# Sparsemax cross-attention and FFN on one core: thresholds tested by exact row sums on ScalarE, projections moved between phases

## The chip, the cores and the metric

One Trainium2 chip, one core of it. The metric is device time in microseconds (us) of one execution, median of several. Engines are named as the profile names them: PE (TensorE), DVE (VectorE), ACT (ScalarE), POOL (GpSimd), SP (SyncE, which here only starts transfers).

## What is computed

Eight batch elements; for each, 100 query rows of width 512 attend over 722 context rows with 16 heads of 32, and a feed-forward block follows. The attention weights are not a softmax but a sparsemax, which needs for every row a threshold tau such that the clipped row sums to one:

```python
def sparsemax(x):
    x = x - jnp.max(x, axis=-1, keepdims=True)
    zs = -jnp.sort(-x, axis=-1)
    cssv = jnp.cumsum(zs, axis=-1) - 1.0
    support = zs > cssv / rho                      # rho = 1, 2, ..., L
    k = jnp.maximum(jnp.sum(support, axis=-1, keepdims=True), 1)
    tau = jnp.take_along_axis(cssv, k - 1, axis=-1) / k
    return jnp.clip(x - tau, 0.0)

x = x + attn(layernorm(x), ctx, ctx, Wq, bq, Wk, bk, Wv, bv, Wo, bo)   # scores * 32**-0.5, sparsemax, @ v, @ Wo
real = layernorm(x) @ cos(theta + theta_noise)
imag = layernorm(x) @ sin(phi + phi_noise)
x = x + sqrt(real * real + imag * imag)
```

## The kernel before, in words

Work goes in half-batches: half `i` holds the 8 heads `8*(i%2)..` of batch element `b = i//2`, so there are 16 halves. Every engine runs its own program in order; they meet at semaphores. The order of work is written out by hand as **phases** `i = -1..17`, and each engine's program has the same loop `for i in PHASES`, with generators that give steps of work and a function `weave` that mixes two of them.

What one half goes through:

- **k, v, q.** PE multiplies the context by `wk2` and `wv2` in three fp16 terms (`three_terms`, L407; 12 matmuls of k or v are one unit of four steps), the normalised x by `wq` in float32 (L445 to L448, after a transpose, L432). ACT reads each result out of PSUM (k twice, as `ks` L605 and `k_f` L609; v, L594, with a cast of the next batch's context, `high_ctx`, right behind it), POOL makes the low fp16 parts (`low_k` L323, `low_ctx` L314, `low_q` L329), SP stacks k in `kst` (`stack_k`).
- **scores(i).** 16 matmuls (L494) give the 8 heads' scores; ACT copies each head to the tile `S` (100x722 float32). `S` holds two halves.
- **maxes(i, h)**, DVE: 12 MAX8 a head (L803) find 96 candidates a row. **thresholds(i)**, DVE: four Newton steps on the candidates of all eight heads (L812 to L837), then a last comparison (L839 to L848) that counts whether the number above tau changed (`n_last`, `n_now`) and whether a piece's eighth candidate is above tau (`n_edge`).
- **sum_flags(i)**, PE: three small matmuls add these counts over the rows into `flag_ps` (L480 to L482). **settle(i)**, DVE: it waits for them, loads their maximum into a register, and if it isn't 0 loops over the eight heads, loads each head's count and refines the heads that are not 0 (`refine`: the row clipped again from `S`, L872, two Newton steps over all 722 elements, L851 to L862, a test whether that was enough). Then it raises `verified`.
- **split_tau(i)**, POOL: after `verified` five small instructions split tau in three fp16 parts (L344 to L352) and raise `tau_split`.
- **attend(i)**, PE: it waits for `tau_split`, transposes the parts (L531), ACT copies them beside q, then six units of transposed scores minus tau (L543), clipped by ACT into `pT` (L711), multiplied with v (L520), woven with k matmuls.
- Then the output projection (`o_of`, L457), the second layernorm, the FFN (L472), `sum_squares`, `root`, `y_of`, and the store.

DVE does half `i` in phase `i`, with `settle(i-1)` after the third head's maxes; PE in phase `i` does `sum_flags(i-1)`, `attend(i-1)` and `scores(i+1)`:

```python
if odd:
    first = chain(q_of(b + 1), k_of(b + 1, 0), k_of(b + 1, 1)) if b + 1 < B else iter(())
    second = ffn_of(b - 1) if 0 <= b - 1 < B else iter(())
else:
    first = chain(k_of(b, 2), k_of(b, 3)) if b < B else iter(())
    second = chain(*vs[0:2], *([o_of(b - 1)] if b > 0 else []), *vs[2:])
```

`first` runs ahead of attend and woven into it, `second` is woven into the scores. In the prologue SP starts all weight transfers, POOL fills constants (L292 to L307), DVE splits the weights and computes the angles of the FFN weights (`angles`).

## Time and profile before

| | |
|---|---|
| median of 3 runs | 979.97 us (978.62 to 981.37) |
| profiled execution, its own time | 981.16 us |
| span in its profile | 979.3 us |
| PE matmuls busy | 600.7 us, 61% |
| DVE busy | 670.2 us, 68% |
| ACT busy | 372.5 us, 38% |
| POOL busy | 185.7 us, 19% |
| mean granted clock of TensorE | 0.803 of full speed |

No engine is busy throughout. The chain that ended last is 39% PE, 24% "issue" (an engine that waits for nothing the profile shows), 18% DVE, 5% ACT, 5% POOL.

### The profile page before, as it was taken

The page shows a single profiled execution, that of the slowest core. Times are in us where ns is not written, and L with a number is a line of the kernel's source. Part 1 is how long each engine was busy: PE and PEld are TensorE (multiplying, and loading weights), DVE is VectorE, ACT ScalarE, POOL GpSimd, SP SyncE. Part 2 cuts the span into 40 slices and gives each one's busy share as a digit, 9 for nine tenths or more (in the row PEclk, how much of TensorE's full clock was granted, in tenths as well). Part 3 has the DMA queues.
Part 4 walks back from the last instruction along what each step waited for, and adds up shares of the span by engine and source line. Part 5 has one row for each costly group of instructions (what it writes and reads, how often), then busy time and mean ns, then how long its engine had stood idle before and what let it go on. Part 6 is the DMA issues. An engine that isn't in the chain of part 4 may idle for free.

```text
span 979.3 us, 14685 instructions
## 1 busy us (share of the span) xinstructions
PE 600.7 (61%) x4592; PEld 354.0 (36%) x4592; DVE 670.2 (68%) x2683; ACT 372.5 (38%) x605; POOL 185.7 (19%) x223
## 2 busy tenths in 40 slices
PE   0556716319619097379747960979155498793675
PEld 0233304106305064246434630555042354462442
DVE  7169957659549494689569964996476787694731
ACT  1242324206306054255425540645143354642231
POOL 9523201002200122012301230022110032110000
PEclk9967857659959699598969995989678698987577
DMA  5552000201102010022003200211002020110000
GB/s 176 169 168 58 20 23 14 72 0 45 27 7 71 23 53 17 18 81 66 18 17 86 61 23 11 71 35 52 23 12 82 1 62 24 46 43 8 1 9 9
DMA packets 33452, 44.10 MB, mean 45 GB/s; under 512 B 8347, under 2 KB 26779, under 8 KB 33376
## 3 DMA queue, kind: packets, MB, share of 16 engines
q1 hardware_dynamic: 33376, 43.18, 15.5%
q8 instruction: 36, 0.59, 0.2%
q14 instruction: 40, 0.33, 0.1%
HBM read 23.77 MB, written 1.64 MB: 26 GB/s over the span
## 4 chain that ended last, share of the span: by engine, by line
PE 39%; issue 24%; DVE 18%; ACT 5%; POOL 5%; DVEq 4%; SPq 2%; DMA 1%; POOLq 0%; ACTq 0%
PE ring L407 17%; DVE cand L803 6%; PE ring L472 5%; PE ring L543 4%; PE mix_bank L520 4%; PE ring L457 3%; PE ring L494 3%; PE ring L445 2%; ACT pT L711 2%; DVEq L900 2%; SPq L231 2%; POOL kst L294 1%; PE ring L531 1%; DVE over L851 1%; DVE dif L818 1%
## 5 line engine op out<-in xcount | busy, mean ns | idle before, releaser
L803 DVE MAX8 cand<-S 100x8 f32<-100x60 f32 (+1 forms) x1536 | 191.3, 206 | 73.9 <-issue 71.8
L531 PE MATMUL ring<-ident,tt 100*3 100x100 f16 x128 | 12.0, 262 | 281.0 <-POOLq L354 281.0
L407 PE MATMUL ring<-ctx,wk 128*128 128x361 f16 x768 | 164.6, 355 | 0.0
L407 PE MATMUL ring<-wv,ctx 128*121 128x512 f16 x576 | 140.8, 388 | 4.4 <-ACT v L594 4.4
L594 ACT ACTIVATE qst<-ring 96x800 f16<-96x800 f32 (+1 forms) x32 | 26.4, 831 | 274.3 <-PE ring L531 273.5
L323 POOL TENSOR_TENSOR ks<-k_f,ks 128x361 f16<-128x361 f32 x64 | 68.0, 1062 | 298.6 <-ACT k_f L609 298.1
L594 ACT ACTIVATE S<-ring 100x722 f32<-100x722 f32 x128 | 97.6, 770 | 57.3 <-PE ring L494 57.2
L531 PEld LDWEIGHTS ring<-ident,tt 100*3 100x3 f16 x128 | 8.4, 106 | 286.4 <-POOLq L354 286.4
L407 PEld LDWEIGHTS ring<-wv,ctx 128*121 128x121 f16 x576 | 78.7, 138 | 50.3 <-issue 8.0
L711 ACT ACTIVATE pT<-ring 121x800 f32<-121x800 f32 x96 | 78.8, 839 | 37.9 <-PE ring L543 37.9
L407 PEld LDWEIGHTS ring<-ctx,wk 128*128 128x128 f16 x768 | 73.6, 108 | 49.8 <-issue 18.0
L543 PEld LDWEIGHTS ring<-qst,kst 99*121 99x121 f16 x768 | 71.5, 172 | 21.8 <-ACT qst L594 10.6
L872 DVE SCALAR_TENSOR_TENSOR dif<-S,tau,zero 100x722 f32<-100x722 f32 x15 | 15.0, 998 | 92.4 <-issue 58.0
L314 POOL TENSOR_TENSOR ctx<-ctx_f,ctx 128x484 f16<-128x484 f32 x48 | 53.9, 1124 | 126.3 <-ACT ctx L594 126.1
L543 PE MATMUL ring<-qst,kst 99*121 99x100 f16 x768 | 75.7, 256 | 2.7 <-ACT qst L594 2.5
L494 PE MATMUL ring<-kst,qst 96*100 96x361 f16 x256 | 65.1, 342 | 19.1 <-DMA kst<-ks 17.1
L520 PE MATMUL mix_bank<-pT,v 121*32 121x100 f32 x1536 | 59.0, 277 | 7.7 <-ACT pT L711 7.5
L605 ACT ACTIVATE ks<-ring,bk_c 128x361 f16<-128x361 f32 x64 | 36.1, 564 | 54.5 <-PE ring L407 54.5
L494 PEld LDWEIGHTS ring<-kst,qst 96*100 96x100 f16 x256 | 32.4, 133 | 67.1 <-issue 30.4
L344 POOL TENSOR_SCALAR t_rest<-tau 100x8 f32<-100x8 f32 x16 | 3.7, 233 | 271.5 <-issue 218.1
L818 DVE TENSOR_TENSOR dif<-cand,tau 100x288 f32<-100x288 f32 (+1 forms) x64 | 51.3, 801 | 2.2
L445 PE MATMUL ring<-wq,xT 128*100 128x512 f32 x64 | 33.9, 658 | 23.3 <-ACT xT L594 23.3
(122 smaller groups left out, 900.3 us busy)
## 6 DMA issues: line engine op xcount, KB each, us to landing
kst<-ks SPq DMA_DIRECT2D x384, 45.1 KB, 1.9
ctx_f<-in_ctx SPq DMA_DIRECT2D x48, 242.0 KB, 3.3
xq<-in_x SPq DMA_DIRECT2D x8, 200.0 KB
xr<-in_x SPq DMA_DIRECT2D x8, 200.0 KB
out_y<-att SPq DMA_DIRECT2D x8, 200.0 KB
S<-in_L_xattn_Wk SPq DMA_DIRECT2D x1, 1024.0 KB, 7.1
wq<-in_L_xattn_Wq SPq DMA_DIRECT2D x1, 1024.0 KB, 9.8
S<-in_L_xattn_Wv SPq DMA_DIRECT2D x1, 1024.0 KB, 7.8
```

What stands on the lines that cost most here:

```text
L314: pool.tensor_tensor(ctx2[:, 1, :, at], ctx_f[:, n % 3, :, :], ctx2[:, 0, :, at], ALU.subtract).then_inc(ctx_lo_ready, 1)
L323: pool.tensor_tensor(ks[:, n % 2, 1, at], k_f[:, half, :], ks[:, n % 2, 0, at], ALU.subtract).then_inc(k_lo_ready, 1)
L407: last = nc.tensor.matmul(psum, lhs(c, i), w(c, j), start=(c == 0 and n == 0), stop=(c == DC - 1 and n == 2))
L445: nc.tensor.matmul(psum, xT[:, c, :], wq[:, c, :], start=(c == 0), stop=False)
L472: last = nc.tensor.matmul(psum, x2T[:, c, :], w[:, c, :], start=(c == 0), stop=(c == DC - 1))
L494: last = nc.tensor.matmul(psum[0:L, half, 0:HALF], qst[0:3 * DH, b % 2, HH * part + h, :], kst[0:3 * DH, i % 3, h, half * HALF:(half + 1) ...
L520: last = nc.tensor.matmul(mix_ps[DH * j:DH * (j + 1), :], v[0:CK, kc, DH * h:DH * (h + 1)], pT[0:CK, st_unit(i, g, c2) % 3, c, j * L:(j + ...
L543: last = nc.tensor.matmul(psum[0:CK, c, j * L:(j + 1) * L], kst[0:99, i % 3, G * g + j, kc * CK:(kc + 1) * CK], qst[0:99, b % 2, HH * part ...
L594: return nc.scalar.activation(dst, src, ACT.Copy, **kw)
L711: nc.scalar.activation(pT[0:CK, u % 3, :, :], src, ACT.Relu).then_inc(two_read, 1)
L803: last = nc.vector.max(cand[:, h, 8 * n:8 * n + 8], S[0:L, HH * (i % 2) + h, cuts[n]:cuts[n + 1]])
L818: n = counted(nc.vector.tensor_tensor(dif[:, :, 0:E].rearrange("p g (n r) -> p g n r", r=ranks), pieces[:, :, :, 0:ranks], t4.broadcast_to ...
```

## The change

1. **The test.** The last comparison of `thresholds` is gone (the tile `tau` becomes `neg_tau`, its negative); its last instruction raises `tau_ready`. ACT gets `check(i)`: eight activations that clip each head's scores in `S` in place, `Relu(S + neg_tau)`, with the row sum as accumulator output, then one that gives the excess over `1 + SUM_TOL` (1e-5). `sum_flags` is one matmul over `excess`. `settle` turns the eight sums in a bit mask; it loads one register, tests eight bits of it in code written out eight times, and refines from the clipped row.
2. **The split.** POOL's `split_tau(i)` waits for `tau_ready` and not for `verified`; PE's `attend` waits for both. After a refinement DVE splits again (`split_again`).
3. **The order.** v chunks 3 to 5 go from the even phase's `second` to the front of the odd phase's `first`; `q_of` goes from the odd phase to the middle of the even phase's `first`; k units are per (m, half); `settle` comes after the sixth head's maxes; `ln1`, `ln2`, `sum_squares`, `y_of`, loads of x and `low_ctx` move with them.
4. **The prologue.** ACT starts five of the weight transfers, the second noise has a place of its own in `S`, DVE makes the low context parts of batch 0, `angles` has six instructions in place of eight, POOL's one large fill of `kst` rows 96 to 98 is cut in three (`fours`), two of them later.

```diff
@@ sync: prologue and loop
-            weight(wk_f, Wk, in_wk)
             weight(wq[:, :, :], Wq, in_wq)
...
-            weight(wcos[:, :, :], theta, in_angle)
-            weight(noise, theta_noise, in_angle)
-            weight(wsin[:, :, :], phi, in_angle)
+            load_xq(1)
+            weight(wv_f, Wv, in_wv)
             load_xr(0)
             stack_k(0, 0)
             stack_k(0, 1)
-            sp.wait_ge(angle_step, 1)
-            weight(noise, phi_noise, in_angle)
...
                     if b < B:
                         stack_k(b, 2)
-                        stack_k(b, 3)
+                    if b + 2 < B:
+                        load_xq(b + 2)
                     if b > 1:
                         store(b - 2)
+                    if b < B:
+                        stack_k(b, 3)
@@ gpsimd
-                pool.wait_ge(verified, i + 1)
+                pool.wait_ge(tau_ready, i + 1)
@@ tensor
                 pe.wait_ge(flag_ready, i + 1)
-                nc.tensor.matmul(flag_ps, ones[:, :], n_last[:, :], start=True, stop=False)
-                nc.tensor.matmul(flag_ps, minus[:, :], n_now[:, :], start=False, stop=False)
-                nc.tensor.matmul(flag_ps, ones[:, :], n_edge[:, :], start=False, stop=True).then_inc(flag_sum, 1)
+                nc.tensor.matmul(flag_ps, ones[:, :], excess[:, :], start=True, stop=True).then_inc(flag_sum, 1)
...
                 pe.wait_ge(tau_split, i + 1)
+                pe.wait_ge(verified, i + 1)
...
-                    first = chain(q_of(b + 1), k_of(b + 1, 0), k_of(b + 1, 1)) if b + 1 < B else iter(())
+                    first = chain(*([v_of(b, kc) for kc in range(KC // 2, KC)] if 0 <= b < B else []),
+                                  *([q_of(0)] if b < 0 else []),
+                                  *([k_of(b + 1, m, half) for half in range(2) for m in range(2)] if b + 1 < B else []))
                     second = ffn_of(b - 1) if 0 <= b - 1 < B else iter(())
                 else:
-                    first = chain(k_of(b, 2), k_of(b, 3)) if b < B else iter(())
-                    vs = [v_of(b, kc) for kc in range(KC)] if b < B else []
-                    second = chain(*vs[0:2], *([o_of(b - 1)] if b > 0 else []), *vs[2:])
-                for _ in range(4):
+                    first = chain(*([k_of(b, 2, 0), k_of(b, 2, 1)] if b < B else []),
+                                  *([q_of(b + 1)] if b + 1 < B else []),
+                                  *([k_of(b, 3, 0), k_of(b, 3, 1)] if b < B else []))
+                    vs = [v_of(b, kc) for kc in range(KC // 2)] if b < B else []
+                    second = chain(*vs[0:1], *([o_of(b - 1)] if b > 0 else []), *vs[1:])
+                for _ in range(16 if odd else 14):
                     next(first, None)
                 if attended:
                     sum_flags(i - 1)
-                for _ in range(10 if odd else 4):
+                for _ in range(4 if odd else 8):
                     next(first, None)
@@ scalar
+            def check(i):
+
+                act.wait_ge(tau_ready, i + 1)
+                for h in range(HH):
+                    row = S[0:L, HH * (i % 2) + h, :]
+                    nc.scalar.activation(row, row, ACT.Relu, bias=neg_tau[:, i % 2, h:h + 1],
+                                         accum_out=row_sum[:, h:h + 1]).then_inc(relu_done, 1)
+                    if h == HH - 1:
+                        act.wait_ge(relu_done, HH * (i + 1))
+                        nc.scalar.activation(excess[:, :], row_sum[:, :], ACT.Relu,
+                                             bias=above[:, :]).then_inc(flag_ready, 1)
+                    yield
...
-                for _ in range(14 if odd else 8):
-                    next(first, None)
+                checks = check(i - 1) if attended else iter(())
+                run(first, 8)
+                if odd and 0 <= b - 1 < B:
+                    ln_sd(b - 1, mv2, sd2, ln2_stat, ln2_sd)
+                if not odd and 0 <= b - 2 < B:
+                    root(b - 2)
+                run(checks, 3)
+                run(first, 4 if odd else 1)
+                run(checks, 3)
+                run(first, 4 if odd else 5)
+                run(checks, 2)
+                run(first, 4 if odd else 8)
@@ vector
-                todo = dve.value_load(any_i[0:1, 0:1], min_val=0, max_val=2 * L * NCAND)
+                todo = dve.value_load(flag_i[0:1, 0:1], min_val=0, max_val=2 ** HH - 1)
                 with dve.If(todo > 0):
-                    with dve.Fori(0, HH) as h:
-                        rows = dve.value_load(flag_i[0:1, bass.ds(h, 1)], min_val=0, max_val=2 * L * NCAND)
-                        with dve.If(rows > 0):
+                    dve.wait_ge(tau_split, i + 1)
+                    for h in range(HH):
+                        with dve.If((todo >> h) & 1 > 0):
                             refine(i, h)
+                    split_again(i)
                 dve.sem_inc(verified, 1)
...
-                    if h == 2 and i > 0:
+                    if h == 5 and i > 0:
                         settle(i - 1)
```

Two places show how the order of instructions moves.

**PE, from the scores of an odd phase to the tau of the next even phase.** L407 and L433 are the k and v matmuls, L445 and L470 the q projection, L480 to L482 and L505 the flags, L531 and L557 the transposed tau. Before:

```order
L494 MATMUL ring<-kst,qst 100x361 x16
L407 MATMUL ring<-ctx,wk 128x361 x12
L480 MATMUL flag_bank<-n_last,ones 1x8
L481 MATMUL flag_bank<-n_now,minus 1x8
L482 MATMUL flag_bank<-n_edge,ones 1x8
L407 MATMUL ring<-ctx,wk 128x361 x12
L531 MATMUL ring<-ident,tt 3x100 x8
L407 MATMUL ring<-ctx,wk 128x361 x3
```

Now:

```order
L517 MATMUL ring<-kst,qst 100x361 x16
L433 MATMUL ring<-ctx,wk 128x361 x24
L457 MATMUL ring<-ident,xq 128x100 x4
L470 MATMUL ring<-wq,xT 100x512 x4
L472 MATMUL ring<-bq,one 100x512
L473 MATMUL ring<-bq,one 100x512
L505 MATMUL flag_bank<-excess,ones 1x8
L433 MATMUL ring<-ctx,wk 128x361 x24
L557 MATMUL ring<-ident,tt 3x100 x8
L569 MATMUL ring<-qst,kst 121x100 x16
```

In the even phase the transpose and the q projection, and all four k units, now stand ahead of tau, and nothing is woven into the attend.

**ACT, the same even phase.** L634 and L638 read k, L735 are the new clipping sums, L739 the excess, L624 the copies. Before (L605 and L609 read k, L683 is `root`):

```order
L605 ACTIVATE ks<-ring,bk_c 128x361
L609 ACTIVATE k_f<-ring,bk_c 128x361
L605 ACTIVATE ks<-ring,bk_c 128x361
L609 ACTIVATE k_f<-ring,bk_c 128x361
L594 ACTIVATE qst<-ring 3x800
L683 ACTIVATE sq<-sq 100x512
```

Now:

```order
L634 ACTIVATE ks<-ring,bk_c 128x361
L638 ACTIVATE k_f<-ring,bk_c 128x361
L712 ACTIVATE sq<-sq 100x512
L735 ACTIVATE S,row_sum<-S,neg_tau 100x722 x3
L624 ACTIVATE xT<-ring 128x400
L735 ACTIVATE S,row_sum<-S,neg_tau 100x722 x3
L624 ACTIVATE qn<-ring 100x16x32 x2
L624 ACTIVATE q_f<-ring 100x512
L735 ACTIVATE S,row_sum<-S,neg_tau 100x722 x2
L739 ACTIVATE excess<-row_sum,above 100x8
```

The eight sums stand between the reads of k, xT and q, so xT is copied behind three sums and the flags are ready only behind the q reads. In an odd phase the order is: reads of v 3 and 4, three sums, v 5, three sums, one k unit, two sums, the excess, one k unit, tau.

## Rows read from the trace of the kernel before

**Rows 1.** The page: busy time, share of the span and instructions of each engine.

```profile
PE 600.7 (61%) x4592; PEld 354.0 (36%) x4592; DVE 670.2 (68%) x2683; ACT 372.5 (38%) x605; POOL 185.7 (19%) x223
```

**Rows 2.** Who waited for whom: us in total, times, longest.

```profile
PE ring L531 <- POOLq L354: 281.0, 16, 34.4
```

**Rows 3.** Groups of instructions by line: busy us, mean ns of one | idle before.

```profile
L872 DVE SCALAR_TENSOR_TENSOR dif<-S,tau,zero 100x722 f32<-100x722 f32 x15 | 15.0, 998 | 92.4 <-issue 58.0 <-remote 34.4
L839 DVE TENSOR_TENSOR over<-cand,tau 100x768 bf16<-100x768 f32 x16 | 15.3, 957 | 0.5
```

**Rows 4.** Timeline of DVE: a settle with one refined head, one with none.

```profile
479.95 0.15 DVE L894 CAST flag_i<-flag_bank 1x8 int32<-1x8 f32 x1 [5.21 <-PE flag_bank L482]
486.75 1.38 DVE L872 SCALAR_TENSOR_TENSOR dif<-S,tau,zero 100x722 f32<-100x722 f32 x1 [6.57 <-issue]
...
501.34 7.45 DVE L803 MAX8 cand<-S 100x8 f32<-100x60 f32 x60 [7.14 <-issue]
...
527.01 0.57 DVE L848 TENSOR_REDUCE n_now<-fold 100x8 f32<-100x400 bf16 x1
...
532.94 0.13 DVE L894 CAST flag_i<-flag_bank 1x8 int32<-1x8 f32 x1
534.49 3.04 DVE L803 MAX8 cand<-S 100x8 f32<-100x60 f32 x24 [1.35 <-issue]
```

**Rows 5.** Timeline of PE around the tau transposes: start, us, instruction, idle before.

```profile
154.88 0.82 PE L531 MATMUL ring<-ident,tt 100*3 100x100 f16 x8 [28.50 <-POOLq L354]
439.72 0.82 PE L531 MATMUL ring<-ident,tt 100*3 100x100 f16 x8 [4.19 <-POOLq L354]
...
453.60 2.80 PE L407 MATMUL ring<-wv,ctx 128*121 128x512 f16 x12
...
476.87 2.82 PE L445 MATMUL ring<-wq,xT 128*100 128x512 f32 x6 [1.23 <-ACT xT L594]
...
481.44 3.86 PE L407 MATMUL ring<-ctx,wk 128*128 128x361 f16 x24
502.97 0.82 PE L531 MATMUL ring<-ident,tt 100*3 100x100 f16 x8 [17.67 <-POOLq L354]
...
536.11 0.82 PE L531 MATMUL ring<-ident,tt 100*3 100x100 f16 x8 [4.53 <-POOLq L354]
...
771.18 0.82 PE L531 MATMUL ring<-ident,tt 100*3 100x100 f16 x8 [24.10 <-POOLq L354]
820.35 0.51 PE L531 MATMUL ring<-ident,tt 100*3 100x100 f16 x8 [3.72 <-POOLq L354]
940.58 0.52 PE L531 MATMUL ring<-ident,tt 100*3 100x100 f16 x8 [3.28 <-POOLq L354]
```

**Rows 6.** Stretches: busy time (x count) of PE, PEld, DVE, ACT, POOL, PEclk, DMA.

```profile
432.00:436.00 4.00, 3.53 (x27) 1.92 (x25) 4.00 (x30) 1.94 (x4) 0.88 (x1) 1.00 0.00 0
440.00:444.00 4.00, 4.00 (x29) 2.73 (x27) 3.97 (x30) 2.51 (x4) 0.00 (x0) 0.50 0.27 70
```

**Rows 7.** Groups of instructions by line, ACT: busy us, mean ns of one.

```profile
L594 ACT ACTIVATE S<-ring 100x722 f32<-100x722 f32 x128 | 97.6, 770 | 57.3 <-PE ring L494 57.2
L609 ACT ACTIVATE k_f<-ring,bk_c 128x361 f32<-128x361 f32 x64 | 35.6, 556 | 0.0
L744 ACT ACTIVATE wcos<-wcos 128x2048 f32<-128x2048 f32 x1 | 1.9, 1909 | 0.0
```

**Rows 8.** Timeline of the prologue, DVE and POOL.

```profile
6.79 9.09 DVE L790 TENSOR_SCALAR xq<-xq,mv,sd 100x512 f32<-100x512 f32 x1
44.41 2.93 DVE L931 TENSOR_TENSOR wcos<-wcos,v 128x2048 f32<-128x2048 f32 x1 [21.52 <-DMA wsin<-in_L_ffn_phi]
68.13 2.29 DVE L931 TENSOR_TENSOR wsin<-wsin,v 128x2048 f32<-128x2048 f32 x1 [7.64 <-DMA v<-in_L_ffn_phi_noise]
83.72 7.45 DVE L803 MAX8 cand<-S 100x8 f32<-100x60 f32 x60
...
0.98 14.61 POOL L294 MEMSET kst<- 3x17424 f16 x1
```

More of the change, by code:

```diff
@@ L64, in build_kernel @@
     PHASES = range(-1, NH + 2)
-    two, one = {}, {}
+    two, one, k_use = {}, {}, {}
     for i in PHASES:
@@ L74, in build_kernel @@
         if odd:
-            if b + 1 < B:
-                use(one, ("xT", b + 1))
-                use(one, ("q", b + 1))
-        for m in (0, 1) if odd else (2, 3):
-            for half in range(2):
-                if b + odd < B:
-                    use(one, ("k", b + odd, m, half))
+            for kc in range(KC // 2, KC):
+                if 0 <= b < B:
+                    use(one, ("v", b, kc))
+            if b < 0:
+                use(one, ("xT", 0))
+                use(one, ("q", 0))
+            if b + 1 < B:
+                for half in range(2):
+                    for m in range(2):
+                        use(one, ("k", b + 1, m, half))
+                        use(k_use, (b + 1, m, half))
+        elif b < B:
+            for m in (2, 3):
+                for half in range(2):
+                    use(one, ("k", b, m, half))
+                    use(k_use, (b, m, half))
+                if m == 2 and b + 1 < B:
+                    use(one, ("xT", b + 1))
+                    use(one, ("q", b + 1))
         if 0 <= i - 1 < NH:
@@ L95, in build_kernel @@
         else:
-            for kc in range(KC):
+            for kc in range(KC // 2):
                 if b < B:
                     use(one, ("v", b, kc))
-                if kc == 1 and b > 0:
+                if kc == 0 and b > 0:
                     use(one, ("o", b - 1))
@@ L384, in _ @@
                     if b + 1 < B:
-                        for kc in range(KC):
+                        for kc in range(3):
                             low_ctx(b + 1, kc)
@@ L580, in _ @@
                         next(second, None)
-                weave(scores(i + 1) if i + 1 < NH else iter(()), second, 1 if odd else 3, 0 if odd else 4)
+                weave(scores(i + 1) if i + 1 < NH else iter(()), second, 1 if odd else 2, 0 if odd else 4)
         @block.scalar
@@ L722, in chain, with weight @@
                     yield from part
+            def weight(dst, src, done):
+                act.dma_start(dst, src.rearrange("(c p) n -> p c n", p=P)).then_inc(done, 16)
+            weight(wk_f, Wk, in_wk)
+            weight(wcos[:, :, :], theta, in_angle[0])
+            weight(noise_c, theta_noise, in_angle[0])
+            weight(wsin[:, :, :], phi, in_angle[1])
+            weight(noise_s, phi_noise, in_angle[1])
             act.wait_ge(dve_const, 1)
@@ L728, in _, with run @@
             act.wait_ge(in_bias, 64)
+            def run(steps, n):
+                for _ in range(n):
+                    next(steps, None)
             for i in PHASES:
@@ L764, in _ @@
                         next(second, None)
-                weave(scores(i + 1) if i + 1 < NH else iter(()), second, 1 if odd else 3, 0 if odd else 4)
+                weave(scores(i + 1) if i + 1 < NH else iter(()), second, 1 if odd else 2, 0 if odd else 4)
             root(B - 1)
@@ L974, in _ @@
                     ln2_stats(b - 1)
-                if odd and b >= 1:
-                    sum_squares(b - 1)
+                if odd and b + 2 < B:
+                    ln1_apply(b + 2)
+            sum_squares(B - 2)
+            y_of(B - 2)
             settle(NH - 1)
-            y_of(B - 2)
             ln2_stats(B - 1)
```

323 lines of the change are left out of this document (174 added, 149 removed).

## The prediction

> **What bounds the kernel now.** I read the page first: no engine is busy more than 68% [rows 1], so the time lies in waits. The list of who waited for whom has one that dwarfs the rest: PE stands 281.0 us in 16 waits before the tau transpose, for POOL's `tau_split` [rows 2]. POOL only passes on what DVE's `settle` releases, so I read DVE around it. A settle with nothing to refine takes from the cast at 532.94 to the next MAX8 at 534.49, 1.55 us; one with a single refined head takes 479.95 to 501.34, 21.4 us [rows 4]. The group of L872 says that 15 heads of 128 were refined, with 92.4 us of idle before them [rows 3]. Third, PE's timeline: the distance from one tau transpose to the next, where nothing is refined, is 49.2 us from an odd to an even phase (771.18 to 820.35) and 33.1 us from an even to an odd one (502.97 to 536.11), 82.3 a batch [rows 5]. Over the 15 distances that would be 8 x 49.2 + 7 x 33.1 = 625; the trace has 940.58 - 154.88 = 785.7. So some **160 us are refinements**, and one or two more of them lie before 154.88. The base is a chain PE, DVE, POOL.
>
> **Part 1a, fewer refinements.** The old test fires when a count changed or a piece's eighth candidate is above tau; the new one only when a row's sum exceeds 1 by 1e-5. I put the reference's inputs through the four Newton steps. The old test fires for 15 heads, by halves 2, 2, 2, 1, 1, 0, 1, 0, 2, 0, 2, 1, 0, 0, 1, 0, the count of L872 [rows 3]. The new one fires for 3: one head in each of halves 1, 3 and 10 (excess 0.007 to 0.025); the largest other excess, in float32, is 1.7e-6. Price of one that stays: 21.4, less the clip of L872 (1.0), less the eight passes of the loop with a register load. The idle 6.57 before L872 with head 4 flagged, against 1.35 in a clean settle, makes a pass (6.57 - 1.35) / 4 = 1.3. In their place eight bit tests of some 0.3, and `split_again`, 1.2: 21.4 - 1.0 - 10.4 + 2.4 + 1.2 = **13.6**. The mask is written out, so DVE's program grows from 1689 to 6105 rows; I take no extra for jumps, at most 5 us each (rival 2).
>
> **Part 1b, the test on ACT.** No clip with a row sum on ACT is in the trace. Two rows bound its duration: ACT with a bias takes 556 ns for 361 elements and 1909 for 2048 [rows 7], a line that gives 845 at 722. Neighbours overlap, the sum must be read out: lower end 0.75, the 770 ns of an S copy [rows 7]; upper end 1.1, what DVE takes for the same with sum (998 ns, L872, and its readout) [rows 3]. I take **0.9 each, 7.2 a half and 0.4 for the excess**. What DVE loses, the last comparison (957 ns of L839 [rows 3] and three smaller ones, some 2.1 a half), is worth nothing by itself: from settle to the end of thresholds DVE needs 19.5 (501.34 to 527.6 less three heads of 1.5 and the comparison [rows 4]) and is then 5 us or more ahead of PE in the sums below. The Trainium skill, ScalarE: Activation LUTs, section What ACT_TABLE_LOAD costs, gives an ACTIVATE with a pointer bias 280 ns + 0.833 ns an element and an overlap of 93 ns; by that, an estimate, a sum takes 0.79 (no price for the readout), and the total would be 0.11 x 8 x 15 = 13 us lower than mine. Its section Rules for kernel authors would give a relu to VectorE; L872's 998 ns for the same elements does not bear that out here.
>
> **Part 2, the split beside the test.** The 1.6 us of POOL's five instructions, and the k halves queued ahead of them, leave the path (33.1 and 49.2 held them).
>
> **Part 3, the order.** The sums stand in ACT's queue between reads that PE waits for. I time a phase from PE's last scores matmul. *Even:* k, 24 matmuls, 3.9 [rows 5], transpose 0.45: PE at 4.35. ACT reads k until 5.1, root 5.7, three sums 8.4, xT 8.9: **PE idles 4.6**. q is 8 pieces of 0.47 [rows 5] and 0.6 of bias, 4.2 at full clock. The clock matters: after the wait of 4.19 the eight tau matmuls take 0.82 and the stretch 440 to 444 has clock 0.50, the low one of the two levels (1.2 GHz); without that they take 0.51, and 432 to 436 has 1.00, 2.4 GHz [rows 5, 6]. So q takes 7.6, to 16.5. ACT: q 18.2, two sums 20.0, excess 20.4; flags 20.6, **PE idle again 4.1**. Four k units, 3.9 to 6.5 by the clock (3.72 before 820.35 left it high, 4.19 did not [rows 5]), I take 5.2: tau at 25.8; `verified` is there at 22.2. Attend without k: 453.60 - 439.72 = 13.9, less k 3.9, less 1 for low clock: 9. Then v, o and scores, 21.5 before (453.60 to 475.1), less 36 v matmuls (7.8), plus 0.6: 14.3. Length 49.1. *Odd:* v 7.9, a k unit: PE at 9.9. ACT: v reads and casts 6.4, 6.7, three sums 9.4, v 5 10.4, three sums 13.1, k 14.1, two sums 15.9, excess 16.3: flags 16.5, **PE idle 6.6**; k 12 matmuls at low clock 3.8: tau 20.3, after `verified` (18.1). From there to the end as before, 502.97 to 527.4, less 0.5: 23.9. So odd to even is 23.9 + 25.8 = 49.7, even to odd 23.3 + 20.3 = 43.6: **93.3 a batch against 82.3**. The new order costs 11 us a batch; it is the missing refinements that pay. A refinement delays tau by 20.6 + 13.6 - 25.8 = 8.4 in an even phase, 16.5 + 13.6 - 20.3 = 9.8 in an odd one: 27, I take 30 with the first jump into that code. SP: `stack_k(b, 3)` is now behind a store that waits for `y_of`, at about 25, when its k is just made: nothing.
>
> **Part 4, the prologue.** Angles wait for noise: phi's at 68.13, maxes(0) at 83.72; theta's part began at 44.41, when six weight transfers of 1 MB and the context had come [rows 8]. Now nothing holds the seventh back; at the same pace it lands by 50 to 54, and six instructions for eight cut each angle pass to 13: maxes(0) at 68. Thresholds(0) end 8 heads and 16.5 later and 1.5 for waits, at 98. DVE's L790 took 9.09 while POOL filled `kst` for 14.6 [rows 8]; the three thirds (4.9 each) may hit DVE anywhere: 0 to 10. The Trainium skill, SBUF — State Buffer, section SBUF: two separate sides, calls the pair of ports of both engines an exclusive lock; that row agrees. Sums, one v, one k and the excess: flags at 108, a k unit at low clock 112. Then ACT has both Sin (1.9 each [rows 7]) and two table loads ahead of tau's copy, which a refinement used to hide: 6 more. Tau(0) counts as **118 instead of 154.9**.
>
> **Sum.** 118 + 7 x 93.3 = 653, - 8 (phase 1 has no FFN), + 30, + 30 from tau(14) to tau(15) (DVE's 19.5, then the sums behind root), + the tail as before, 979.3 - 940.6 = 38.7: 862 of span, against 979.3. The profiled execution took 1.9 more than its span, and the median lies 1.2 under it: **862**.
>
> **The rivals.**
> 1. *Gaps that cost no clock.* For: 4.5 us of wait before 536.11, but only 3.7 before 820.35 with tau at 0.51 [rows 5]. Against: 0.50 after 4.19 [rows 6]. A batch is then 86.0, the time 862 - 7 x 7.3 = **811 to 816**.
> 2. *Long sums, dear jumps.* Sums of 1.1 cost 0.2 x 8 x 15 = 24; a clean settle that jumps over 300 rows and takes 5 us more passes its slack (3.6 in an even phase, 2.2 in an odd one): 13 x 1.1 at 6 even and 2.8 at 7 odd, some 28. Together up to **900 to 914**. The 1.35 of idle after a short jump [rows 4] neither shows nor excludes it.
> 3. *Rounding makes the exact test fire.* ACT's sum adds 722 float32 values in its own order; if that errs by more than 1e-5 where I have 1.7e-6, clean halves are refined. With one head in all 13 others it costs 13 x 9.1 = 118: **980, the point from which it is slower**; with two heads, 8.5 more each, **1090**. Against: my own float32 sums.
> 4. *The test saves nothing:* the same 15 heads refined, seven settles more at 9.1 and five second heads at 8.5: 862 + 106 = **968**.
>
> **How the numbers follow.** Forecast 0.55, rival 1 0.22, rival 2 0.17, rival 3 0.03, rival 4 0.03. The range 812 to 902 holds the forecast, most of rival 1 and of rival 2; it leaves out their ends, and 3 and 4. A measurement of this kernel tells 0.3% from no change, 3 us: faster 0.96, the same 0.01, slower 0.03.
>
> **What would show it.** Right: L919 twice per refined head, 3 heads; ACT's clip with sum 128 times near 0.9 us; in even phases PE idle 4 to 5 us before q, for xT, and about 4 before the flags; in odd ones 6 to 7 before the flags; little idle before tau (L557); tau to tau 44 and 50 us; first MAX8 near 68. Wrong: more than 3 refined heads, PE waiting at L557 for DVE in clean phases (jumps, or thresholds late), sums over 1.1, clock near 1 after the gaps.

## The result and the profile after

| | before | after |
|---|---|---|
| median | 979.3 us (977.66 to 981.37, 4 runs) | **918.13 us** (916.68 to 920.59, 4 runs) |
| ratio | | 0.9377, 95% interval 0.9347 to 0.9407 |
| span in the profile | 979.3 us | 918.8 us |
| mean granted clock | 0.803 | 0.827 |

Faster by 6.2%, but 56 us slower than the 862 forecast and outside the range, which ended at 902. Medians below are over all executions of a run; where some lie over 1.5% above the fastest (two of E2's four), the comparison goes by the others. From the page of the kernel after, the engines and, from its fourth part, the chain that ended last by engine:

```profile
PE 636.9 (69%) x4528; PEld 368.0 (40%) x4528; DVE 540.5 (59%) x2390; ACT 488.4 (53%) x877; POOL 167.6 (18%) x218
...
PE 50%; ACT 22%; SPq 13%; issue 9%; DMA 4%; POOL 1%; DVE 0%; ACTq 0%; POOLq 0%
```

Beside [rows 1], DVE lost 130 us of work and ACT gained 116. DVE has left the chain, where it had 18%. SPq, the queue of the engine that only starts transfers, has grown in it from 2% to 13%. The prediction gives it nothing.

Who waited for whom, kernel after (us in total, times, longest); rows in the order of the list:

```profile
PE flag_bank L505 <- ACT excess L739: 88.2, 16, 9.4
...
PE ring L557 <- issue: 55.2, 12, 14.6
...
PE ring L517 <- DMA kst<-ks: 41.1, 16, 7.8
...
PE ring L470 <- ACT xT L624: 26.4, 7, 4.3
```

The 281.0 us before the tau transpose [rows 2] are gone. Four smaller waits stand there, 211 in all: for the flags and for `xT`, both forecast; at the transpose (L557), forecast for refined halves only; and for `kst`, the stacked k, not forecast. Two of the four are not new: the kernel before waited 23.3 for `xT` and 17.1 for `kst`, but 13.6 of that 17.1 lay in the prologue. Of the 41.1 now, 13.1 lie there; the others come at most two at a time, between the tau of an odd phase and that of the even one. The groups of the new test in the kernel after (count | busy, mean ns | idle before):

```profile
L735 ACT ACTIVATE S<-S,neg_tau 100x722 f32<-100x722 f32 x128 | 113.1, 890 | 0.0
...
L735 ACT ACTIVATION_READ_ACCUMULATOR S<-S,neg_tau 100x1 f32 x128 | 24.9, 195 | 0.0
...
L919 DVE SCALAR_TENSOR_TENSOR S<-S,delta,zero 100x722 f32<-100x722 f32 x6 | 6.4, 1065 | 0.0
```

Six L919 are three heads, two steps each: three refined heads, as forecast, against 15.

One undisturbed batch of the kernel after, PE's timeline (start, us, count; in brackets the idle time before and what ended it). It answers to [rows 5]:

```profile
440.13 0.20 PE L505 MATMUL flag_bank<-excess,ones 100*1 100x8 f32 x2 [6.17 <-ACT excess L739]
440.26 3.74 PE L433 MATMUL ring<-ctx,wk 128*128 128x361 f16 x12
444.27 0.51 PE L557 MATMUL ring<-ident,tt 100*3 100x100 f16 x8 [0.27 <-issue]
...
463.27 0.47 PE L517 MATMUL ring<-kst,qst 96*100 96x361 f16 x2
463.58 1.02 PE L497 MATMUL ring<-wsin,x2T 128*100 128x512 f32 x2
467.29 0.51 PE L517 MATMUL ring<-kst,qst 96*100 96x361 f16 x2 [2.69 <-DMA kst<-ks]
467.64 1.84 PE L497 MATMUL ring<-wsin,x2T 128*100 128x512 f32 x2
...
481.34 5.37 PE L470 MATMUL ring<-wq,xT 128*100 128x512 f32 x8 [4.29 <-ACT xT L624]
...
491.00 0.20 PE L505 MATMUL flag_bank<-excess,ones 100*1 100x8 f32 x2 [3.74 <-ACT excess L739]
491.13 5.54 PE L433 MATMUL ring<-ctx,wk 128*128 128x361 f16 x24
496.60 0.52 PE L557 MATMUL ring<-ident,tt 100*3 100x100 f16 x8
...
540.34 0.51 PE L557 MATMUL ring<-ident,tt 100*3 100x100 f16 x8 [0.67 <-issue]
```

The three gaps are as forecast (6.17, 4.29, 3.74 against 6.6, 4.6, 4.1), and 496.60 to 540.34 is 43.7 (forecast 43.6). But 444.27 to 496.60 is 52.3 and not 49.7: at 467.29 the scores of the fifth head wait for `kst`, and the FFN pair behind the wait takes 1.84 in place of 1.02. SP's timeline over the same stretch, kernel after:

```profile
450.15 5.63 SPq L246 DMA_DIRECT2D kst<-ks  x8
455.82 2.49 SPq L250 DMA_DIRECT2D kst<-ks  x4
458.41 4.99 SPq L246 DMA_DIRECT2D kst<-ks  x8
463.44 2.49 SPq L250 DMA_DIRECT2D kst<-ks  x4
```

And two pieces of its chain of waits there (start, us, what):

```profile
464.70 0.59 SPq L250
...
465.34 1.91 DMA kst<-ks
```

SP starts 24 transfers one behind the other, 450.15 to 465.93, 0.66 us each, and the last needs 1.91 to land. Only then can PE go on.

A refinement, DVE's timeline of the kernel after, phase 2:

```profile
163.26 0.15 DVE L961 SCALAR_TENSOR_TENSOR flag_bits<-flag_bank,bit 1x8 f32<-1x8 f32 x1 [17.59 <-PE flag_bank L505]
...
170.21 0.91 DVE L908 TENSOR_SCALAR_CACHE_REDUCE over<-S 100x722 bf16<-100x722 f32 x1 [6.60 <-issue]
...
176.68 0.15 DVE L936 CAST again_i<-again_m 128x1 int32<-128x1 f32 x1
180.75 0.17 DVE L947 TENSOR_SCALAR t_rest<-neg_tau 100x8 f32<-100x8 f32 x1 [3.92 <-remote]
```

and PE beside it:

```profile
163.16 5.54 PE L433 MATMUL ring<-ctx,wk 128*128 128x361 f16 x24
182.11 0.82 PE L557 MATMUL ring<-ident,tt 100*3 100x100 f16 x8 [13.41 <-issue]
```

The head's own work takes 6.6 us; 6.60 and 3.92 us of idle lie before and behind it.

### The profile page after: what moved, and what is told of

The parts are those of the page before. It is cut to its first block, busy times and chain, and to the rows that moved or that the text cites. A ratio compares the mean times of both kernels' runs of the same rounds, so it can differ in the third digit from the quotient of the medians.

```text
span 918.8 us, 13839 instructions
## 1 busy us (share of the span) xinstructions
PE 636.9 (69%) x4528; PEld 368.0 (40%) x4528; DVE 540.5 (59%) x2390; ACT 488.4 (53%) x877; POOL 167.6 (18%) x218
## 3 DMA queue, kind: packets, MB, share of 16 engines
q1 hardware_dynamic: 30736, 37.94, 14.9%
## 4 chain that ended last, share of the span: by engine, by line
PE 50%; ACT 22%; SPq 13%; issue 9%; DMA 4%; POOL 1%; DVE 0%; ACTq 0%; POOLq 0%
PE ring L433 24%; ACT S L735 10%; SPq L246 9%; PE ring L569 5%; PE ring L470 5%; PE ring L497 4%; SPq L250 4%; PE mix_bank L543 4%; PE ring L517 4%; PE ring L482 3%; ACT pT L755 2%; DMA bo_b<-in_L_xattn_bo 2%; DMA kst<-ks 2%; ACT k_f L638 2%; ACT qst L624 1%
## 5 line engine op out<-in xcount | busy, mean ns | idle before, releaser
L433 PE MATMUL ring<-ctx,wk 128*128 128x361 f16 x768 | 164.4, 370 | 0.0
L433 PE MATMUL ring<-wv,ctx 128*121 128x512 f16 x576 | 139.0, 393 | 0.0
L624 ACT ACTIVATE S<-ring 100x722 f32<-100x722 f32 x128 | 96.6, 769 | 79.5 <-PE ring L517 79.5
L334 POOL TENSOR_TENSOR ks<-k_f,ks 128x361 f16<-128x361 f32 x64 | 59.4, 929 | 354.3 <-ACT k_f L638 354.0
L735 ACT ACTIVATE S<-S,neg_tau 100x722 f32<-100x722 f32 x128 | 113.1, 890 | 0.0
L433 PEld LDWEIGHTS ring<-ctx,wk 128*128 128x128 f16 x768 | 80.6, 112 | 58.3 <-issue 19.1
L433 PEld LDWEIGHTS ring<-wv,ctx 128*121 128x121 f16 x576 | 79.6, 139 | 46.7 <-issue 7.7
L517 PE MATMUL ring<-kst,qst 96*100 96x361 f16 x256 | 67.2, 359 | 42.9 <-DMA kst<-ks 41.1
L634 ACT ACTIVATE ks<-ring,bk_c 128x361 f16<-128x361 f32 x64 | 35.9, 561 | 88.0 <-PE ring L433 88.0
L326 POOL TENSOR_TENSOR ctx<-ctx_f,ctx 128x484 f16<-128x484 f32 x42 | 47.8, 1138 | 182.8 <-ACT ctx L624 182.7
L569 PEld LDWEIGHTS ring<-qst,kst 99*121 99x121 f16 x768 | 66.8, 170 | 34.2 <-ACT qst L624 22.0
L470 PE MATMUL ring<-wq,xT 128*100 128x512 f32 x64 | 42.0, 818 | 42.6 <-ACT xT L624 26.4
L543 PE MATMUL mix_bank<-pT,v 121*32 121x100 f32 x1536 | 63.6, 293 | 9.5 <-ACT pT L755 8.6
L505 PE MATMUL flag_bank<-excess,ones 100*1 100x8 f32 x32 | 3.2, 171 | 88.2 <-ACT excess L739 88.2
L624 ACT ACTIVATE v<-ring 121x512 f32<-121x512 f32 x48 | 28.5, 594 | 53.4 <-PE ring L433 53.4
L624 ACT ACTIVATE qst<-ring 96x800 f16<-96x800 f32 (+1 forms) x32 | 26.4, 830 | 55.1 <-PE ring L557 54.2
L883 DVE TENSOR_TENSOR dif<-cand,neg_tau 100x288 f32<-100x288 f32 (+1 forms) x64 | 50.9, 795 | 2.2
## 6 DMA issues: line engine op xcount, KB each, us to landing
kst<-ks SPq DMA_DIRECT2D x384, 45.1 KB, 1.9
```

The source lines that it names most:

```text
L334: pool.tensor_tensor(ks[:, n % 2, 1, at], k_f[:, u % 2, :], ks[:, n % 2, 0, at], ALU.subtract).then_inc(k_lo_ready, 1)
L433: last = nc.tensor.matmul(psum, lhs(c, i), w(c, j), start=(c == 0 and n == 0), stop=(c == DC - 1 and n == 2))
L470: nc.tensor.matmul(psum, xT[:, c, :], wq[:, c, :], start=(c == 0), stop=False)
L517: last = nc.tensor.matmul(psum[0:L, half, 0:HALF], qst[0:3 * DH, b % 2, HH * part + h, :], kst[0:3 * DH, i % 3, h, half * HALF:(half + 1) ...
L543: last = nc.tensor.matmul(mix_ps[DH * j:DH * (j + 1), :], v[0:CK, kc, DH * h:DH * (h + 1)], pT[0:CK, st_unit(i, g, c2) % 3, c, j * L:(j + ...
L569: last = nc.tensor.matmul(psum[0:CK, c, j * L:(j + 1) * L], kst[0:99, i % 3, G * g + j, kc * CK:(kc + 1) * CK], qst[0:99, b % 2, HH * part ...
```

## The experiments

Two terms of the sum were in doubt once the profile was read: the order of the k units with SP's queue behind it, and the price of a refinement. The runs take each away, then both, then ask what the new test costs when it never fires. Medians are of four or five runs, those of the kernel before beside them 978.72 to 980.04.

**E1: k by m.** In the tables and in the programs of PE, ACT and POOL:

```diff
-                for half in range(2):
-                    for m in range(2):
+                for m in range(2):
+                    for half in range(2):
...
-    *([k_of(b + 1, m, half) for half in range(2) for m in range(2)] ...
+    *([k_of(b + 1, m, half) for m in range(2) for half in range(2)] ...
```

> The changed kernel with the k units of the odd phase in the old order (both halves of m = 0, then both of m = 1) on PE, ACT and POOL; nothing else. Theory 1 (the 24 transfers of 0.63 us each that SP issues behind the second half of m = 0 are what I missed): the 41 us that PE waits for the k transfers fall to some 15, all in the prologue, and the time falls by 20 to 35 us, to 883 to 898. Theory 2 (settle's long code): the waits for transfers fall too, but others take their place and the time falls by less than 8. Theory 3 (the sums on ACT bound it): the same, less than 8.

Measured: **886.3 us** (884.16 to 887.47), ratio 0.9051 (0.9031 to 0.9071), 31.8 less than the change. Who waited, kernel of E1:

```profile
PE flag_bank L505 <- ACT excess L739: 90.5, 16, 9.4
...
PE ring L517 <- DMA kst<-ks: 15.1, 7, 5.6
```

The wait for `kst` falls by 26.0, its occasions from 16 to 7; the flags' wait stays. `kst` for m = 0 needs both halves of its k, and by halves the second one comes third, inside attend: the first transfer of a batch starts 5.9 us after tau (450.15 - 444.27), in E1 0.7 after it (SP's first row there stands at 431.10, tau at 430.42). The odd to even distance falls from 52.3 to 48.5. The order of the k units cost some 32 us, with the same transfers in both. The time lies inside the expected 883 to 898.

**E3: never refine.** Left out in E3, E4, E5 and E9: the refinement, so heads that need it keep their tau. The sums and the flags stay.

```diff
-                with dve.If(todo > 0):
+                with dve.If(todo > 255):
```

> The changed kernel with the refinement's condition out of reach (mask > 255), so the three heads that need it keep their tau; test, code and jumps stay. My prediction gave the three refinements 27 to 30 us. Theory 2: each settle with one takes 18.6 us from flag to tau where I had 13.6, so 40 us or more, 878 or less. Otherwise 885 to 895.

Measured: **853.75 us** (853.0 to 859.61), ratio 0.872 (0.8705 to 0.8734): 64.4 us less than the change, where the prediction has 30 for all three refinements. This run takes away more than them. From its waits, and a clean settle of its DVE timeline:

```profile
PE ring L557 <- issue: 2.3, 2, 1.2
```

```profile
404.92 3.04 DVE L868 MAX8 cand<-S 100x8 f32<-100x60 f32 x24 [0.77 <-DVE flag_i L964]
```

The idle behind a clean settle's cast is 0.77 us here and 3.55 to 4.06 in the change, though the edit was meant to leave the code and its jump in place. The register can't hold more than 255 (its `max_val`), so the condition is never true and the block may be missing from the program; why the jump is short stays open. So E3 removes three refinements and the long jump of the 13 other settles. Of the 55.2 us at L557, 40.8 are the three refined halves (13.41, 12.75, 14.63) and 14.4 are nine clean ones, 10.6 of these in the last three halves, where little or no k work stands behind the flags. What a refinement cost by itself is read from tau to tau: the halves 1, 3 and 10 lengthen the distance before them by 12.8, 14.2 and 14.9 and the one behind them by 5.4, 6.1 and 2.3, together 55.7, or 18.6 each. Part of that lies in the attend behind the wait. A table of stretches (us, busy PE, PEld, DVE, ACT and POOL with counts, granted clock, DMA share, GB/s), from tau to the end of attend, in the change, after a wait of 13.41:

```profile
182.00:195.00 13.00, 11.68 (x152) 9.18 (x152) 12.41 (x50) 6.18 (x8) 0.00 (x0) 0.50 0.00 1
```

and in E3, without it:

```profile
168.60:178.20 9.60, 6.96 (x153) 5.43 (x152) 9.22 (x23) 6.99 (x10) 2.15 (x2) 1.00 0.20 50
```

0.50 is the low level, 1.2 GHz, and 1.00 the high one, 2.4 GHz: the same attend takes 3.4 us more at the low one.

**E4: no block.** `settle` loads its register and the refinement's code is gone from the program:

```diff
-                with dve.If(todo > 0):
-                    dve.wait_ge(tau_split, i + 1)
-                    for h in range(HH):
-                        with dve.If((todo >> h) & 1 > 0):
-                            refine(i, h)
-                    split_again(i)
```

> As the kernel that never refines, but without the refinement's code: settle loads the mask and raises verified at once. It prices the jump over some 300 rows alone. A clean settle takes 3.9 us from flag to the next MAX8 in the changed kernel and 1.55 in the kernel before. Theory 2: 2.3 us less in each of 16 settles, and where tau waits for it the time falls by 10 to 35 us against the one with the jump. Theories 1 and 3: in most phases a k unit hides it, less than 8 us.

Measured: **856.33 us** (855.16 to 857.24), ratio 0.8744 (0.8728 to 0.876), 2.6 over E3. It was to price the jump over the code, and it can't: E3 has no long jump either (idle behind the cast 0.77, in E4 0.71). The jump has to be read in the change itself. Kernel after, DVE in a clean settle:

```profile
440.56 0.14 DVE L964 CAST flag_i<-flag_code 1x1 int32<-1x1 f32 x1
444.26 3.04 DVE L868 MAX8 cand<-S 100x8 f32<-100x60 f32 x24 [3.56 <-issue]
```

3.70 from the cast to the next MAX8, against 1.55 [rows 4]. PE's k unit behind the flags ends at 444.00 and hides all but 0.27 of it. A clean batch of E1, which has the jump, takes 92.0 (430.42 to 522.40), one of E9, without it, 92.1: in mid-kernel it costs nothing on the path. In the last three halves PE waits 2.27, 4.22 and 4.14 for it. The pages' rows of the instruction queue, the first of the change, the second the same in E3 and in E4:

```profile
q14 instruction: 69, 0.56, 0.2%
```

```profile
q14 instruction: 35, 0.28, 0.1%
```

In the change one 8 KB packet of this queue starts inside the idle of each of the 12 clean settles that run on into a MAX8 (at 442.37 in the one shown), some 2 us after the cast or a little less, and DVE goes on 1.4 to 1.6 us after it has ended. In E3 none of the 15 such settles has one.

**E9: k by m, never refine.** E1 and E3 together.

```diff
+                for m in range(2):
+                    for half in range(2):
...
+                with dve.If(todo > 255):
```

> The changed kernel with the old order of k units and with no refinement, both causes at once. If the 32 us of the k order and the 64 us of the refinements are two separate things, it is 918 - 96 = 822 (my own sum without refinements was 862 - 30 = 832). If they overlap, above 835.

Measured: **827.15 us** (826.43 to 828.14), ratio 0.8438 (0.8424 to 0.8453). Adding the two gains gives 918.1 - 31.8 - 64.4 = 821.9; the two terms are nearly independent (E3 less E9 is 26.6 for the order, the change less E1 31.8). The forecast without its 30 of refinements is 832. PE's timeline of E9:

```profile
392.61 0.52 PE L557 MATMUL ring<-ident,tt 100*3 100x100 f16 x8
...
441.54 0.52 PE L557 MATMUL ring<-ident,tt 100*3 100x100 f16 x8
...
484.70 0.52 PE L557 MATMUL ring<-ident,tt 100*3 100x100 f16 x8
```

48.9 and 43.2, 92.1 a batch: the forecast's 93.3 fits the order in which SP's queue costs nothing, as it had assumed.

**E5: the kernel before, never refining.**

```diff
-                with dve.If(todo > 0):
+                with dve.If(todo > 19200):
```

> The kernel before with the refinement's condition out of reach (count > 19200), so its 15 refined heads keep their tau; tests and order stay. It prices the 15 refinements and gives the old order without them. My prediction had 160 us of them behind the first tau and one settle with two heads (31) before it: 785 to 800. If each costs its wait and then a stretch at low clock, as the runs with the changed kernel suggest, it is the same number, since the trace of before held both: so under 775 or over 815 would say the clean distances of 49.2 and 33.1 were read wrongly. Compared with the changed kernel that never refines (854) it says what the new order costs.

Measured: **760.5 us** (760.39 to 763.56), ratio 0.776 (0.7747 to 0.7773), below the expected 785 to 800 and under the 775 that was to speak against the reading of the clean distances; 67 under E9. Its wait at the tau transpose:

```profile
PE ring L531 <- POOLq L354: 59.7, 16, 4.0
```

So the 15 refinements of the kernel before cost some 219 us, 14.6 each (with a little for the clean settles, whose idle of 0.96 to 1.35 is 0.77 in E5, as in E3), and not 160 plus one or two: 192 lie between first and last tau (785.7 against 594.1) and 24.6 before the first (154.88 against 130.26). The clean distances of the prediction do recur (295.30 to 329.53 is 34.2, 329.53 to 379.32 is 49.8), but its 625 took all 15 as full ones; those at the two ends, with less work in them, are shorter (36.1 the first, 38.6 and 27.4 the last two).

**E2: short sums.** Each sum takes 2 of 722 columns, so no head is ever refined, and the scores are not clipped in place.

```diff
-   nc.scalar.activation(row, row, ACT.Relu, bias=neg_tau[:, i % 2, h:h + 1],
+   nc.scalar.activation(row[:, 0:2], row[:, 0:2], ACT.Relu, bias=neg_tau[:, i % 2, h:h + 1],
```

> The changed kernel with each of the 128 clipping sums over 2 elements of its row in place of 722, so the test always passes, and no head is refined: exactness is left out. A sum costs some 0.3 us in place of 0.88, so 4.6 us less a half in ACT's queue. Theory 3: the waits before q, before the flags and in the odd phases shrink by what the sums shrink: 16 x 4.6 = 74 us, and more from the clock, below the kernel without refinement. Theory 1: transfers take over part of it, 30 to 50 us below that kernel.

Measured: **831.0 us** (823.12 to 838.36), and 824.5 for the comparison, a rough figure. Against E3 that is 29 less, a little short of the expected 30 to 50 and far from 74. Waits of E2:

```profile
PE flag_bank L505 <- ACT excess L739: 38.5, 16, 4.6
PE ring L557 <- issue: 28.6, 13, 4.6
```

50 us less of waiting for flags (88.3 in E3) buy 29. But the two differ in the jump too: E2 has it in each settle, with idle of 3.6 to 4.0, and PE waits 28.6 at L557 against 2.3.

**E12: the same on E1's order.**

```diff
+                for m in range(2):
+                    for half in range(2):
...
+   nc.scalar.activation(row[:, 0:2], row[:, 0:2], ACT.Relu, bias=neg_tau[:, i % 2, h:h + 1],
```

> The changed kernel with the old order of k units and each sum over 2 elements, so no refinement and no exactness: it prices the 128 sums with nothing but the rest of the new order left. Without refinement the kernel with full sums takes 827, the old order 760. If the sums are the difference (16 x 4.6 = 74 less what still costs 0.3 each): 765 to 775. If their places in ACT's queue and the settle after six heads hold the rest: 785 to 805.

Measured: **794.36 us** (788.42 to 797.57), ratio 0.8117 (0.8084 to 0.8151) and inside the expected 785 to 805: 33 under E9, 34 over E5. The taus split the 67 us that E9 takes over E5. The first tau comes at 109.71 in E9 and at 130.26 in E5, so the new prologue gives back 20.6. From first to last tau E9 takes 677.0, E12 639.5 and E5 594.1: the new order costs 82.9 there, short sums remove 37.5 of them, though E12 has the long jump and E9 has not, and 45.4 stay with the short sums themselves, the jump and the places of q, v and settle, which no run took apart.

**E6: xT first.** ACT reads `xT` ahead of the first three sums, not behind them.

```diff
-                run(first, 8)
+                run(first, 8 if odd else 9)
...
-                run(first, 4 if odd else 1)
+                run(first, 4 if odd else 0)
```

> The changed kernel with the copy of xT ahead of the first three sums on ACT in even phases. PE's wait before q (26 us in 7 phases) goes; q runs at the high clock, the flags wait stays near 4. Theory (sums between the reads): 7 x 4 to 6 = 25 to 45 us less, 873 to 893. Rival (the flags are bound by ACT's sums anyway, so the wait only moves to the flags): under 12 us less.

Measured: **901.36 us** (896.66 to 905.62), ratio 0.9182 (0.9153 to 0.9211), 16.8 less than the change, between the expected 25 to 45 and the rival's 12. Waits of E6:

```profile
PE flag_bank L505 <- ACT excess L739: 95.7, 16, 9.4
...
PE ring L470 <- ACT xT L624: 8.1, 7, 1.2
```

18.3 off the wait for `xT`, 7.5 more for the flags: part of the gap only moves to the next thing that ACT has late.

**E7: both orders.** E1's lines and E6's.

```diff
+                for m in range(2):
+                    for half in range(2):
...
+                run(first, 8 if odd else 9)
...
+                run(first, 4 if odd else 0)
```

> Both order changes together, exact and with refinements: old order of k units, xT ahead of the sums. If the gains add: 886 less 25 to 45, so 841 to 861; rival: 875 or more.

Measured: **871.13 us** (863.22 to 874.83), ratio 0.8902 (0.8879 to 0.8925): 15.2 under E1, against 16.8 that E6 gives alone. These also add, but with E6's smaller gain, so the time lies between the expected 841 to 861 and the rival's 875.

**E10: E7 with more candidates.** 14 pieces of the row in place of 12, so that MAX8 finds more of what belongs to the sum. Refined is then one head, in half 3.

```diff
-PIECES = 12
+PIECES = 14
```

> The changed kernel with the old order of k units, xT ahead of the sums, and 14 pieces of a row in place of 12, exact. From the reference's inputs the exact test then fires for 1 head in place of 3 (half 3), at 16 more MAX8 a half (some 1.8 us) and thresholds a sixth longer on DVE, which has slack. Theory (a refinement costs its wait of 13 and a stretch at low clock of 5 to 7, about 20 together): 871 less 40, 825 to 838. Rival (the slack of DVE is used up, thresholds become the last to arrive): 850 or more.

Measured: **831.3 us** (830.58 to 832.83), ratio 0.8486 (0.8463 to 0.8509), inside the expected 825 to 838. Two heads fewer are 39.8 us, 20 each net of MAX8's longer work. Both kernels have the long jump in their clean settles, which E3 had not, and the price is near the 18.6 read from tau to tau. E10 is well ahead of the kernel before and of the change.

**E8: E10 with the eight sums in one block.** In even phases all sums stand behind `xT` and ahead of q's reads.

```diff
-                run(first, 4 if odd else 5)
+                run(first, 4 if odd else 0)
...
-                run(first, 4 if odd else 8)
+                run(first, 4 if odd else 13)
```

> As the kernel with 14 pieces, with all eight sums of a half in one block: in even phases behind xT and ahead of the q read, in odd phases behind the read of v 4. The flags are ready some 1 to 2 us earlier a phase, q, v 5 and k are read later. Theory (ACT's queue ahead of the flags is the path): 5 to 20 us under the run with the sums in three blocks. Rival (the reads that PE needs come later and give it back): within 4.

Measured: **829.01 us** (821.2 to 833.05), ratio 0.8474 (0.8431 to 0.8516). Not to be told from E10, as the rival had it (within 4); with it the fastest of the kernels that leave nothing out, 15% under the kernel before.

**E11: the kernel before with 14 pieces.** The same line; refined are 6 heads in 6 halves.

> The kernel before with 14 pieces in place of 12, nothing else. The old test then fires for 6 heads in 6 halves in place of 15 in 10. A refinement costs some 220 / 15 = 14.6 us here (980 to 760), more where it is alone in its half (some 20): 760 + 6 x 20 = 880, plus up to 4 us a half for MAX8 and thresholds where DVE is the last to arrive: 880 to 930. If under 870, refinements cost less alone than I think.

Measured: **872.45 us** (867.86 to 876.95), ratio 0.8918 (0.8881 to 0.8956), a little under the expected 880 to 930. One number in the old kernel beats the whole change. With it and the two orders mended, the changed kernel as a whole is 41 us ahead (E10); that takes in its prologue and one refined head against six, so it isn't the worth of the new test.

## Why the prediction was wrong, and where it was right

Its sum term by term, with the measured value from the profiles of the change, E3 and E9 (tau is the start of the transpose):

| term | forecast | measured | from |
|---|---|---|---|
| first tau | 118 | 111.2 | the change |
| first to fifteenth tau, clean | 645 | 642.2 | E9, 109.71 to 751.86 |
| order of k, SP's queue | 0 | 32.8 | E3, 110.50 to 785.45, less E9 |
| three refinements, and the long jump | 30 | 56.4 | the change, 111.17 to 842.49, less E3 |
| fifteenth to last tau | 30 | 37.0 | the change, to 879.46 |
| tail | 38.7 | 39.3 | the change |
| span | 862 | 918.8 | |

Two rows need a word. E3's profiled execution (859.61) is the slowest of its five, and two distances in it (360.35 to 407.44 to 462.39) are 6.3 longer together than their like. So some 26 of the 32.8 belong to the order of k and some 63 to the row below: 55.7 for the refinements, some 7 for the jump in clean settles. And the clean row is in part luck: E9's first distance is 55.3 where the forecast has 41.7 (5.97 of it is the stall for the two Sin, which the forecast counts in the first tau), and its fourteenth tau comes 39.7 after the thirteenth, where the forecast has 49.7, with a q projection that the last batch no longer has. The two misses nearly cancel; the batches between them, 92.1 each, are right.

**Part 3's last sentence failed:** SP "nothing", because the k of m = 3 is "just made" when the store is past. I asked when the queue comes to the work, not how long it needs, and I looked at m = 3, where nothing went wrong. The change also turned m-by-m into half-by-half for m = 0 and 1; I counted those k units for PE and priced none of the 24 transfers behind them: 0 in the sum, 27 (E3 less E9) to 32 (the change less E1) on the chip. The kernel before held the price. Its SP timeline, the second stack of a batch:

```profile
514.16 4.94 SPq L231 DMA_DIRECT2D kst<-ks  x8
519.14 2.49 SPq L235 DMA_DIRECT2D kst<-ks  x4
```

That is 7.5 us of issuing a stack. Two of them, 15 us, can't be through within the attend in which they now begin (444.27 to 455.97 in the change). E1, with the transfers begun 0.7 us after tau, confirms it.

**Part 1a's price of a refinement was half of the measured one,** 10 against 18.6. Its count was exact: three heads, halves 1, 3 and 10 (rival 3, rounding that fires the test, and rival 4, the same 15 heads, are out). From flags to the split tau it has 13.6: 10.0 of work, 2.4 of bit tests, 1.2 of split. The trace has 163.26 to 181.75, 18.5: 0.3 for the register's value, 6.6 idle, 6.6 of work, 3.9 idle, 1.0 of split. The forecast's 10.0 held 6.4 of work (486.75 to 494.20, less the clip, in the kernel before) and some 3.3 of idle behind it, for the loads that ask whether to go on. So the work is as forecast, and the idle of bit tests, loads and jumps is 10.5 in place of 5.7: 4.8 us more. "I take no extra for jumps, at most 5 us each" names the right size and takes the other end. The second half of the error is that the delay was counted up to tau only: PE stood 13 us and ran the attend at clock 0.50, 3.4 us more, with more behind it. [rows 5] had it too: 0.82 for the eight transposes after every long wait.

The Trainium skill, Runtime: NRT & Kernel Launch, section Instruction fetch mechanics, says that a taken branch whose target lies outside the window of fetched pages waits for a transfer of that page. The trace agrees: idle behind the clean settle's jump grew from 1.35 to 3.56 as the code jumped over grew, a packet of the instruction queue starts inside each such idle, and two (165.66 and 168.06) inside the 6.60 before the refined head's work. No run varied the length of the jump alone, and the packets' row doesn't name the engine they serve, so the link rests on these times. The 3.92 behind the head's work has no such packet in it. Rival 2's dear jumps in clean settles came in part: 2.2 to 2.7 us more each in place of 5, and some 9 us of the span (7 between the first and the fifteenth tau, 2 behind) in place of 28. Its sums of 1.1 are out.

**Part 1b was right.** Sums follow each other every 0.88 us (forecast 0.9), as ACT's timeline of the change shows:

```profile
478.16 0.89 ACT L735 ACTIVATE S<-S,neg_tau 100x722 f32<-100x722 f32 x1
478.95 0.20 ACT L735 ACTIVATION_READ_ACCUMULATOR S<-S,neg_tau 100x1 f32 x1
479.04 0.89 ACT L735 ACTIVATE S<-S,neg_tau 100x722 f32<-100x722 f32 x1
```

**Part 3's phases were right** for the order by m: gaps, their length and 93.3 a batch (92.1 in E9). q behind its gap took 5.9 with its bias (481.34 to 487.26), between the forecast's 7.6 at the low clock and 4.2 at the high one; the k matmuls behind the flags took 5.54 (forecast 5.2). Rival 1, gaps that cost no clock, would need 86.0 a batch and is out. A batch costs 9 more than in the old order, 92.1 against the 83.2 from 246.33 to 329.53 in E5 (forecast 11).

**Part 4 came out close.** The first MAX8 starts at 60.74, not 68, but the thresholds end only at 93.5 (I had 98): 32.8 in place of 30, since DVE's rows stretch beside POOL's work, the longest of them beside the second third of `kst`. The rest of that lead is lost before the flags, at 106.95 where I had 108. Kernel after, POOL's row and two of DVE, the second the same instruction one step later:

```profile
79.38 4.93 POOL L319 MEMSET kst<- 3x5808 f16 x1
```

```profile
82.01 2.72 DVE L887 TENSOR_SCALAR over<-dif 100x768 bf16<-100x768 f32 x1
...
90.21 0.56 DVE L887 TENSOR_SCALAR over<-dif 100x768 bf16<-100x768 f32 x1
```

The text allowed 0 to 10 for that. First tau is at 111.17 (I had 112 before the stall) and the stall for the two Sin is 4.60, before 117.62 (I had 6). The table counts it in the next term: with it the prologue is 115.8 against 118, and without its 5.97 in E9 the next term is 636 against 645.

**The stretch to the last tau** was 30 in the sum and took 37.0; 35.2 in E3 and 34.9 in E9, so about 2 of the 7 are the jump and 5 were missing in the term itself. No run took it apart. The sum's line "118 + 7 x 93.3 = 653" gives the product alone; its end, 862, is added up rightly.

**The base was read wrong, and it did not show.** 160 us for the refinements of the kernel before were 219. The sum was built from the new phases, so the misreading never entered it; but 219 over 15 heads, 14.6 each, would have spoken against my 9 to 10.

**The range** took only what I had named as unknown: sums, jumps in clean settles, clock. Both failed terms were points without bounds: a queue at nothing, and three refinements at 9 to 10 each, with a bound of 5 for the jump that the 902 does not hold.

## What to carry over

When a step moves, count the transfers that hang on it and multiply by what its queue takes to issue one (here 24 by 0.66 us); a consumer waits for the last. Price a rare path by taking it away on the chip, and look in the trace whether only it has gone; or else count the wait and the low clock behind it, not its instructions. Before adding work to every round to make a test exact, ask whether the old one can be made to fire less: more candidates took 107 us off the old kernel (E11), the whole change 61.

## What the runs showed of the hardware

- SP needs 0.59 us and a pause of 0.04 to start one `kst` transfer, 45.1 KB from SBUF to SBUF; eight and four take 4.99 and 2.49. The bytes don't set it: `xr`, 200 KB, was started in 0.51 (465.97), a store of 200 KB in 0.32 (497.31). The Trainium skill, DMA: Bandwidth & Descriptors, section Anatomy of one DMA, gives some 50 ns for the dispatch and 2.0 us fixed per transfer, for a path that another engine starts. The landing of 1.91 agrees; the 0.59 is no 50 ns, and here the measurement decides.
- An attend at granted clock 0.50 took 13.0 us and at 1.00 9.6: half the clock, a third more time, with ACT busy 6.2 and 7.0 us in it.
- A wait removed need not be worth its length: 50 us less for the flags gave 29 (E2 against E3, with the jump back in E2), 18 less for `xT` gave 17 with 7 more elsewhere (E6), while 26 less for `kst` gave 32, with the low clock behind it (1.84 for 1.02 at 467.64) gone too (E1).
